# A prologue rearranged: first stacks loaded by two queues, their pads by a third, fills and scalings at other times, and twenty identity products ahead of the first transposes

## The reference, cut to what matters

```python
x = x + attention(layernorm(x), Wq, Wk, Wv, Wo)        # window of 128, 8 windows
x = x + ffn(layernorm(x), w_up_q, w_up_scale, ...)     # w = (q - 7.5) * scale + lora_a @ lora_b
x = x + delta_block(layernorm(x), ...)                 # norm weights, convolution, scan over time
x = x + ffn(layernorm(x), ...)
```

## Time and profile before

| | |
|---|---|
| median of 3 runs | 1250.92 us (1247.12 to 1251.68) |
| profiled execution | 1251.17 us |
| its span in the trace | 1249.3 us |
| mean granted clock of TensorE | 0.915 of full |
| PE busy | 1054.5 us (84%) |
| DVE busy | 920.8 us (74%) |
| ACT busy | 497.3 us (40%) |
| start of the first `scores(0, 0)` | 72.7 us from the span's start |

### The profile page before, as it was taken

The page is one execution under the profiler, slowest core; times in us unless marked ns, Lnnn a source line. Parts: engine busy times, 40 slices in busy tenths (PEclk is TensorE's granted clock), DMA queues, the critical chain, the costliest instruction groups (busy, mean ns, idle before and its releaser), DMA issues.

```text
span 1249.3 us, 22021 instructions
## 1 busy us (share of the span) xinstructions
PE 1054.5 (84%) x8593; PEld 720.7 (58%) x8600; DVE 920.8 (74%) x2425; ACT 497.3 (40%) x1027; POOL 166.5 (13%) x251
## 2 busy tenths in 40 slices
PE   3689879967998999999989999899989988966567
PEld 2355645544556665766666755676566646744445
DVE  2823277898789778887888778977898688968911
ACT  2034254316443554336532653355442634441122
POOL 2000000040003000400040000300040004010400
PEclk9579879987999999889998999999998989987768
DMA  9823013302420134012510233014400210020000
GB/s 279 155 39 79 12 41 99 61 1 77 98 47 1 43 105 76 7 35 79 93 24 9 78 87 56 1 41 109 78 4 27 80 17 1 18 76 0 1 25 9
DMA packets 93608, 67.69 MB, mean 54 GB/s; under 512 B 47233, under 2 KB 86337, under 8 KB 93505
## 3 DMA queue, kind: packets, MB, share of 16 engines
q1 hardware_dynamic: 88544, 60.75, 21.0%
q10 hardware_dynamic: 4960, 5.54, 1.6%
HBM read 45.55 MB, written 20.32 MB: 53 GB/s over the span
## 4 chain that ended last, share of the span: by engine, by line
PE 50%; DVE 27%; ACT 10%; DMA 5%; SPq 4%; issue 3%; POOL 1%; ACTq 0%; DVEq 0%; POOLq 0%
PE bank L1595 7%; PE bank L1487 5%; PE bank L1740 5%; PE bank L1667 4%; PE bank L1749 4%; PE bank L1575 4%; PE bank L1546 4%; PE bank L1580 3%; PE bank L1692 3%; DVE state L1219 3%; DVE lane_buf L1197 3%; PE bank L1541 2%; DVE state L1211 2%; DVE u_l L1206 2%; DVE mx L1007 2%
## 5 line engine op out<-in xcount | busy, mean ns | idle before, releaser
L699 ACT ACTIVATE probs<-bank 128x512 f32<-128x512 f32 x256 | 152.0, 597 | 194.8 <-PE bank L1580 194.4
L1595 PE MATMUL bank<-probs,v_ext 128*9 128x128 f32 x2048 | 161.4, 278 | 13.8 <-ACT probs L699 7.3
L1007 DVE TENSOR_REDUCE mx<-bank 128x2 f32<-128x320 f32 x256 | 120.9, 487 | 57.8 <-PE bank L1546 52.0
L339 POOL TENSOR_TENSOR lane_buf<-state,q_l 128x128 f32<-128x128 f32 x128 | 79.6, 655 | 349.7 <-DVEq L1226 349.7
L1595 PEld LDWEIGHTS bank<-probs,v_ext 128*9 128x9 f32 x2048 | 83.4, 91 | 55.6 <-issue 20.1
L1740 PE MATMUL bank<-feat_c,wgu 128*128 128x256 f32 (+1 forms) x384 | 95.0, 398 | 21.3 <-DVE hid_c L1268 15.7
L1575 PE MATMUL bank<-tri_mask,identb 128*128 128x512 bf16 x256 | 102.0, 399 | 1.4 <-DMA q_stack<-m_rows 1.4
L1580 PE MATMUL bank<-q_stack,k_stack 128*128 128x128 bf16 x1024 | 101.7, 223 | 0.0
L1541 PE MATMUL bank<-edge_mask,identb 128*128 128x64 bf16 x512 | 62.0, 206 | 46.4 <-DVE mx L1007 32.0
L1580 PEld LDWEIGHTS bank<-q_stack,k_stack 128*128 128x128 bf16 x1024 | 80.9, 100 | 34.0 <-issue 4.3
L1197 DVE TENSOR_TENSOR lane_buf<-state,til 128x128 f32<-128x128 f32 x256 | 84.3, 329 | 17.0 <-POOL lane_buf L586 10.2
(11 more groups left out here) (167 smaller groups left out, 1753.1 us busy)
## 6 DMA issues: line engine op xcount, KB each, us to landing
k_pieces<-conv SPq DMA_DIRECT2D x48, 128.0 KB, 2.3
k_stack<-k_pieces SPq DMA_DIRECT2D x32, 192.0 KB
k_stack<-k_pieces SPq DMA_DIRECT2D x32, 128.0 KB
k_l<-lane_k SPq DMA_DIRECT2D x8, 512.0 KB, 3.7
q_l<-lane_q SPq DMA_DIRECT2D x8, 512.0 KB, 5.7
q_pieces<-conv SPq DMA_DIRECT2D x24, 128.0 KB, 2.1
q_stack<-q_pieces SPq DMA_DIRECT2D x32, 96.0 KB
tok<-in_x SPq DMA_DIRECT2D x8, 256.0 KB, 3.2
```

Source lines behind the costliest of these rows:

```text
L699: act.activation(probs[:, u % 2], score_bank[u % 2][:], ACT.Exp, scale=float(DK) ** -0.5).then_inc(exp_done, 1)
L1007: dve.tensor_reduce(mx[:, g, 2 * v:2 * v + 2], bank[1 + u % 2][:, 0:2 * SPAN].rearrange("p (h k) -> p h k", h=2), AX.X, ALU.max).then_inc( ...
L1595: last = pe.matmul(bank[5][row:row + VE, col:col + W], v_ext[:, b, kb, h, :], probs[:, u % 2, (hp * 2 + kb) * W:(hp * 2 + kb + 1) * W], st ...
```

## The change

`load_stacks` and `load_pad` are as before but take the queue, and `load_pad` the semaphore, as arguments. The three stacks of window 0 are issued by two queues: SP takes those of groups 0 and 2, ACT that of group 1. Their pads are issued by POOL, on a semaphore of their own, and PE waits for all six before the first unit. Of the nine piece DMAs of window 0, SP keeps the six of the keys and ACT issues the three of the queries. DVE fills `k_stack` ahead of its wait for the zeroed tiles and adds to `q_stack` after it. DVE scales the delta block's weights after the maxima of groups 0 to 2 and not before them; PE waits for it in `beta_in(0)` and not ahead of the maxima. PE runs WARM = 20 products of the identity with itself ahead of the first transposes.

```diff
+WARM = 20
+        def load_stacks(queue, n, g):
...
+        def load_pad(queue, n, r, landed):
...
+            def first_keys():
+
+                for p, cast in enumerate((piece1, piece2, piece3)):
+                    sp.wait_ge(cast, 2)
+                    for late in range(2):
+                        sp.dma_start(k_pieces[late, :, :, 2 - p, :, 1 - late].rearrange("h b p t -> p (h b) t"),
+                                     pieces[:, 1, p, :].rearrange("p (a t) -> p a t", t=W)).then_inc(pieces_out, 16)
...
             load_residual(0)
-            pieces_to_dram(0)
+            first_keys()
             sp.wait_ge(pieces_out, 144)
             sp.wait_ge(pad_out, 48)
             sp.wait_ge(stack_init, 2)
-            for g in range(RING):
-                load_stacks(0, g)
-                load_pad(0, g)
+            load_stacks(sp, 0, 0)
+            load_stacks(sp, 0, 2)
...
             pool.sem_clear(gstep)
+
+            pool.wait_ge(stack_init, 2)
+            for r in range(RING):
+                load_pad(pool, 0, r, first_pads)
...
             for s in range(2):
                 piece_third(0, s)
+            act.wait_ge(piece3, 2)
+            for p in range(3):
+                act.dma_start(q_pieces[0, :, :, p].rearrange("h b p t -> p (h b) t"),
+                              pieces[:, 0, p, :].rearrange("p (a t) -> p a t", t=W)).then_inc(pieces_out, 16)
             act.wait_ge(zeroed, 6)
             values_out(0)
+            act.wait_ge(pieces_out, 144)
+            act.wait_ge(pad_out, 48)
+            act.wait_ge(stack_init, 2)
+            load_stacks(act, 0, 1)
...
+            done(dve.memset(k_stack[:], 0.0))
+            dve.wait_ge(consts_in, 16 * len(consts))
+            dve.tensor_scalar(k_stack[:], k_stack[:], stack_cols[:, 1:2], None, ALU.add).then_inc(stack_init, 1)
             dve.wait_ge(zeroed, 6)
-            dve.wait_ge(consts_in, 16 * len(consts))
             dve.wait_ge(pad_out, 48)
             dve.tensor_scalar(q_stack[:], q_stack[:], stack_cols[:, 0:1], None, ALU.add).then_inc(stack_init, 1)
-            done(dve.memset(k_stack[:], 0.0))
-            dve.tensor_scalar(k_stack[:], k_stack[:], stack_cols[:, 1:2], None, ALU.add).then_inc(stack_init, 1)
...
+            for g in range(DONE_EARLY):
+                for u in range(g * UPG, (g + 1) * UPG):
+                    max_unit(0, u)
+                max_pieces(0, g)
+
             dve.wait_ge(weights_in, 16 * (len(plain) + IT))
             for k in range(KT):
                 for w, i in ((wqkv_b[:, k], 0), (wbeta[:, k], 0), (wout_b[:, k], 1), (wgu[:, k], 2)):
                     last = dve.tensor_scalar(w, w, norm_w[:, i, k:k + 1], None, ALU.mult)
             last.then_inc(weights_scaled, 1)
-            for g in range(DONE_EARLY):
-                for u in range(g * UPG, (g + 1) * UPG):
-                    max_unit(0, u)
-                max_pieces(0, g)
...
-                    if n == 0 and g < RING:
+                    if n == 0 and g == 0:
+                        pe.wait_ge(first_pads, RING * CHUNK // (2 * W) * 16)
+                    elif n == 1 and g < RING:
                         pe.wait_ge(pad_in[r], 32)
-                    elif n == 1 and g < RING:
-                        pe.wait_ge(pad_in[r], 64)
...
             def beta_in(n, front):
+                if n == 0:
+                    pe.wait_ge(weights_scaled, 1)
...
             pe.wait_ge(early_in, 16 * (len(early) + 2))
+            for _ in range(WARM):
+                pe.matmul(bank[0][:, 0:128], ident[:], ident[:], start=True, stop=True)
             turn_next(0)
...
             pe.wait_ge(lora_added, FT // 2)
-            pe.wait_ge(weights_scaled, 1)
```

More of the change, by code:

```diff
@@ L226, in layer_program @@
         stack_init = sem("stack_init")
+        first_pads = sem("first_pads")
         sq_rstd = sem("sq_rstd")
@@ L346, in terms_of @@
             return last
+        def load_stacks(queue, n, g):
+            b, hh = divmod(g, HH)
+            r = slot(n, g)
+            queue.dma_start(q_stack[MROW:MROW + 3, r], a["zero_rows"]).then_inc(stacks_in[r], 16)
+            for row, m in STACK_ROWS:
+                rows = slice(row * DK, (row + m) * DK)
+                queue.dma_start(q_stack[rows, r].rearrange("p h t -> p (h t)"),
+                                q_pieces[n, hh, b, 0:m].rearrange("p (d h) t -> (p d) (h t)", d=DK)
+                                ).then_inc(stacks_in[r], 16)
+                queue.dma_start(k_stack[rows, r, :, 0:CHUNK],
+                                k_pieces[n, hh, b, 3 - m:3].rearrange("p (d c e) k t -> (p d) c (e k t)", d=DK, c=KC)
+                                ).then_inc(stacks_in[r], 16)
+        def load_pad(queue, n, r, landed):
+            for e in range(CHUNK // (2 * W)):
+                queue.dma_start(k_stack[PADROW:PADROW + 1, r, :, 2 * W * e:2 * W * (e + 1)],
+                                a["pad_row"][:, n * W:(n + 2) * W].rearrange("a (o t) -> a o t", o=1)
+                                .broadcast_to([1, KC, 2 * W])).then_inc(landed, 16)
         def x2(n):
@@ L387, in load_residual @@
                 sp.dma_start(x_in[:], x_v[n:n + 1].rearrange("n p b d -> (n p) b d")).then_inc(x_again, 16)
[L389 to L407, removed]
             def next_stacks(n, g):
                 sp.wait_ge(scores2, (n * NG + g - RING + 1) * UPG)
-                load_stacks(n, g)
+                load_stacks(sp, n, g)
                 if n == 1 and g < RING:
-                    load_pad(1, slot(n, g))
+                    load_pad(sp, 1, slot(n, g), pad_in[slot(n, g)])
+            def first_keys():
[4 more added lines that the diff above has]
+                                     pieces[:, 1, p, :].rearrange("p (a t) -> p a t", t=W)).then_inc(pieces_out, 16)
             def pieces_to_dram(n):
```

## The result

The changed kernel takes 1256.96 us in the median of 11 runs (1251.55 to 1259.16), the kernel before, beside it, 1250.34 (1245.86 to 1255.08). The ratio is 1.005, 95% interval 1.0033 to 1.0066: 4 to 8 us slower, where 2.5 us faster was forecast, and outside the forecast's range of 1244.5 to 1253.2. The profiled execution took 1259.16 us, the longest of the 11; its span is 1257.1 us.

The account below looks back on a forecast made before the run. The prologue's transfers up to stack 0 were taken as the bound. First unit +0.5 us and no pauses between groups -3.1 made the last unit 2.7 earlier: 1251.17 becomes 1248.5, given as 1248.4, range 1244.5 to 1253.2.

Parts of the forecast that it names:

- What bounds the kernel: Prologue, before `scores(0, 0)` at 72.7 us: the transfer chain to stack 0 (51.2) ends last, 1.5 us after compute.
- The stacks on two queues: Prologue loads: stacks 0 and 1 both land at 51.7 us, the third at 57.0; first unit +0.5 us.
- two queues gain nothing: Rival for the stack loads: first unit at 57.1 us, last at 72.2, +2.7 us, 1253.7 in all; chance 0.15.
- The sum's 15.1 us for 24 units: End of prologue: 24 units without a pause take 15.1 us, from 51.7 to 66.8; removed pauses give -3.1.
- The identity products: PE ahead of the transposes: 20 products take at most 4.4 us from 5.6, clock 1.2 GHz again afterwards; value 0.
- the change touches nothing behind: Everything after the prologue: assumed untouched by the change, so only the start of `scores(0, 0)` was asked for.
- DVE's order: DVE in the prologue: fill of `k_stack` and its addition move into idle time, ending at 25.5 us; gain 0.
- the scaling: DVE, moved behind the last maxima: statistics of x some 3.7 us later in DVE's order, 2.7 us margin; cost 0.
- ACT's three issues: Query pieces on ACT ahead of `values_out(0)`: three issues take 2.3 us, 2.1 are free; cost about 0.2.
- POOL's pads: Six pad issues on POOL before the units: about 4 us for six, POOL needed at about 50; cost 0.
- the 40.2 us for the pieces: Landing of the last key pieces in the prologue: forecast unchanged at 40.8 us, bounds 0 and 2.7 us earlier.
- ACT was not stuck: Rival at ACT's DMA issues: they keep ACT until 35.6 us, last unit at 70.2, +0.7, 1251.7; chance 0.05.

## Why the prediction was wrong

*What bounds the kernel*: right for the prologue. Stack 0 ends the last wait, compute is ready 10 us before it (46.0 against 56.05).

*The stacks on two queues*: the step that failed. "The engines stood at 0.67 over the 23.6 us ... which is 15.8 us of full engines, 5.3 for each stack", and so 51.7 for the first unit. The share of busy engines was read as work that could be packed closer. It was packed closer, 0.90 to 0.93, and moved 100 GB/s, where one queue with the same work moved 106. The 90 GB/s of the earlier trace rows, too, came from a single trace, lower than other traces of the same program. First unit 56.05, with stacks 0 and 1 both there, so the rival "two queues gain nothing" (57.1) was right in its mechanism and nearly right about that unit; it had 0.15 and needed most of the chance. Its time, 1253.7, is still 3.3 us short of what was measured, since it knew nothing of the second cost. The rule of the Trainium skill that I cited for it, in "DMA: Bandwidth & Descriptors", "Issuing engines are not separate DMA queues", agrees with these runs: a second queue gave no higher rate (100 GB/s against 106 from one), and the kernel paid because the stack that was wanted first had to share.

The Trainium skill's page "SBUF — State Buffer", section "Door 1: The DMA port swizzle", which I had left out, says that a tile on partitions 0 to 63 reaches 8 of 16 ports. The stacks lie on partitions 0 to 47. But the same section gives 196 GB/s for such a tile in a transfer of 1 MiB, and in the two stretches compared above no trace of before's or the changed kernel moved more than 111, so the ports alone do not account for the rate. No run here moved the stacks to other partitions; what limits them is not shown.

*The sum's 15.1 us for 24 units* was mis-sized: 16.9 (72.95 - 56.05), and 16.4 in two other runs with no wait for stacks between groups. Between groups the four small instructions that split the maxima stand in DVE's way to the next maxima, and PE waits for it (the 0.50 in front of the line at 62.99). Before, the waits for stacks had hidden that.

*The identity products*: the value 0 for the prologue was right: a pause until 16.77 and slow products on L1522. That the clock fell ahead of 16.77 is partly luck: in the six traces with 20 early products it fell between 16.1 and 17.6, and in two of them the transposes at 16.7 still ran fast (0.66 us and not 1.1). Their length was wrong: 6.66 us and not 4.4. The row of four from which 0.22 us was taken is of transposes, which leave one record each; a product of fp32 leaves two, with a weight load each (40 and 40 for the 20). So one takes twice that: 19 records lie in the 4.1 us up to 9.7 and 21 in the 2.5 us behind, 0.43 us for a product at 1.2 GHz and 0.24 at 2.4. The granted clock stood at 2.4 GHz from 9.7 to 16.5.

The second step that failed is the assumption above it, "the change touches nothing behind" the prologue: the products cost 4.6 us in the kernel before, behind a start of attention that is before's. The forecast costed instructions by their time on the engine, and none by the place that they take in its program.

*The rest held*: DVE's order (`k_stack` filled by 26.7, forecast 25.5), the scaling (done at 78.0, statistics ready at 79.0, used at 82.2), ACT's three issues, POOL's pads and the 40.2 us for the pieces cost and gave nothing. ACT was not stuck.

*The sum by the runs*: in the kernel before, the second queue alone costs 7.3 us (ratio 1.0058) and the products alone 4.6, 11.9 together; both with the rest of the change cost 4.1 to 8.3. So the two do not simply add up. With one queue the products cost 3 to 4 us (1.0027 against 1.0002 and 0.9992), with two 0.4 by the ratios. PE's program in the changed kernel differs from before's by a few waits too, and how the two effects combine is not resolved.

*What stays open* is how the number of instructions turns into time. The runs show that 80 instructions cost, that 256 do not, and that the pieces of PE's program come at other moments. No idle time of PE around 365 us names such a piece, and neither the fall of the clock there nor the mean clock follows the cost. The forecast's path behind the prologue is known to be wrong; by what it is lengthened is not known.

## What to carry to other kernels

A low share of busy DMA engines is no free room: look at what rate the transfers reach when they do overlap, in a run that differs in nothing else, and load first, alone, the tile that is waited for first. Work put into an engine's pause is not free because it ends in time: it lengthens the program, and a kernel of thousands of instructions can lose more behind it than the pause was worth. To tell such an effect from one of the work itself, replace the work by as many idle instructions, and count in the trace that they survived the build. Before a single trace's fall of the clock is called a cause, look whether slow and fast kernels differ in it.

## What the runs showed that I had not expected

- Packets of 4 KB and 1 KB to the stacks on 48 partitions moved 106 and 107 GB/s from one queue and 101 and 100 from two, at engine shares of 0.74 and 0.93 against 0.90 and 0.93: a higher share did not mean a higher rate.
- 80 more instructions at the head of PE's program cost 0.36% (0.22 to 0.50) of a program of 1250 us; with 256 more it was 0.03% (from 0.14% less to 0.20% more). The latter is one run.
- In the changed kernel's trace the clock rose when the 20 products had run for 4.1 us, and it fell 4.3 us after they had ended, sooner than the 5.5 us that I had taken from the earlier trace rows.
